# Turning the probabilities of short query blocks in pairs, with zero-padded copies of v, and a new order of all steps

## Time and profile before

| | us |
|---|---|
| median of 3 runs | 584.26 (583.56 to 584.96) |
| the profiled execution | 582.71 |
| its span in the profile | 580.9 |
| PE busy | 528.3 (91%) |
| DVE busy | 448.6 (77%) |
| ACT busy | 413.1 (71%) |
| POOL busy | 349.5 (60%) |

### The profile page before, as it was taken

How to read it: one execution, slowest core, us unless ns; L and a number is a source line. 1 busy time by engine, 2 the same in 40 slices (tenths; PEclk the granted TensorE clock), 3 DMA queues, 4 the chain that set the end, 5 groups by cost and what they waited for, 6 DMA issues and landing times.

```text
span 580.9 us, 22355 instructions
## 1 busy us (share of the span) xinstructions
PE 528.3 (91%) x8180; PEld 451.6 (78%) x8180; DVE 448.6 (77%) x2842; ACT 413.1 (71%) x1004; POOL 349.5 (60%) x358
## 2 busy tenths in 40 slices
PE   4676768999999999999999999999999999989953
PEld 3454647888888888888888888888888888868841
DVE  2799887897897997999998979888989899322114
ACT  3788768867777687867877677778866787566541
POOL 3568456974538565755566645756475648575762
PEclk9678788999999999999999999999999999999995
DMA  7453441000001000110003000200010000000000
GB/s 203 140 173 121 149 143 40 21 2 21 3 3 38 21 3 2 39 39 2 4 2 94 3 3 3 57 21 3 3 39 21 2 21 2 2 19 2 2 18 18
DMA packets 21949, 21.85 MB, mean 38 GB/s; under 512 B 1872, under 2 KB 19792, under 8 KB 21840
## 3 DMA queue, kind: packets, MB, share of 16 engines
q1 hardware_dynamic: 21840, 20.42, 11.5%
HBM read 18.32 MB, written 2.10 MB: 35 GB/s over the span
## 4 chain that ended last, share of the span: by engine, by line
PE 41%; POOL 7%; DVE 5%; issue 4%; ACT 1%; POOLq 0%; DVEq 0%; ACTq 0%
PE ps_o L867 15%; PE ps_z L851 14%; POOL h_lo L522 4%; PE ps_misc L746 3%; PE ps_pt L814 3%; POOL acc L543 2%; PE ps_s L794 2%; PE ps_misc L824 1%; PE ps_misc L754 1%; PE ps_misc L729 1%; DVE taken L959 1%; DVE next L954 1%; ACT h_raw L670 1%; DVE gate_part L998 0%; POOL rstd L561 0%
## 5 line engine op out<-in xcount | busy, mean ns | idle before, releaser
L522 POOL TENSOR_TENSOR h_lo<-h_raw,h_hi 128x512 f16<-128x512 f32 x128 | 148.6, 1161 | 109.1 <-ACT h_raw L670 106.9
L867 PE MATMUL ps_o<-w_hi,h_lo 128*128 128x256 f16 x512 | 139.8, 273 | 5.7 <-POOL h_lo L522 4.9
L851 PE MATMUL ps_z<-x1t_hi,w_lo 128*128 128x256 f16 x512 | 140.5, 274 | 0.1
L851 PE MATMUL ps_z<-x1t_lo,w_hi 128*128 128x256 f16 x512 | 140.1, 274 | 0.0
L851 PE MATMUL ps_z<-x1t_hi,w_hi 128*128 128x256 f16 x512 | 140.0, 273 | 0.0
L867 PE MATMUL ps_o<-w_hi,h_hi 128*128 128x256 f16 x512 | 139.6, 273 | 0.0
L867 PE MATMUL ps_o<-w_lo,h_hi 128*128 128x256 f16 x512 | 139.6, 273 | 0.0
L666 ACT ACTIVATE h_hi<-ps_z 128x512 f16<-128x512 f32 x128 | 75.8, 592 | 69.2 <-PE ps_z L851 69.2
L959 DVE MATCH_REPLACE8 taken<-next,taken 128x64 f32<-128x64 f32 (+4 forms) x480 | 110.6, 243 | 0.2 <-issue 0.2
L543 POOL TENSOR_TENSOR acc<-go_sb,acc 128x512 f32<-128x512 f32 x56 | 71.4, 1275 | 31.1 <-ACT go_sb L680 30.9
L954 DVE MAX8 next<-taken 128x8 f32<-128x64 f32 (+4 forms) x480 | 85.4, 244 | 0.0
(11 more groups left out here) (138 smaller groups left out, 1001.2 us busy)
## 6 DMA issues: line engine op xcount, KB each, us to landing
w_raw<-in_w1t SPq DMA_DIRECT2D x8, 512.0 KB, 4.0
w_raw<-in_w2t SPq DMA_DIRECT2D x8, 512.0 KB, 5.0
xt_sb<-in_xt SPq DMA_DIRECT2D x8, 256.0 KB, 4.2
x_sb<-in_x SPq DMA_DIRECT2D x8, 256.0 KB, 3.4
xa_sb<-in_xt SPq DMA_DIRECT2D x7, 256.0 KB, 3.2
out<-out_sb SPq DMA_DIRECT2D x7, 256.0 KB, 3.5
ctx_sb<-in_ctx_w SPq DMA_DIRECT2D x8, 128.0 KB, 2.2
itok_sb<-in_itok SPq DMA_DIRECT2D x8, 128.0 KB, 2.8
```

The source lines that it names most:

```text
L522: nc.gpsimd.tensor_tensor(h_lo[:, e % 2, 2 * z:2 * z + 2, :], h_raw[:, z, :, :], h_hi[:, e % 2, 2 * z:2 * z + 2, :], ALU.subtract)\
L851: last = pe.matmul(ps_z[z][:, d * UT:(d + 1) * UT], w[:, e, c, at:at + P], x[:, c, :], start=n == 0, stop=n == len(terms) - 1)
L867: last = pe.matmul(ps_o[e % 2][:, b * D:(b + 1) * D], h[:, e % 2, c, b * SEQ:(b + 1) * SEQ], w[:, e, c, :], start=n == 0, stop=n == len(te ...
```

## The change

- `turn_probs`, half 0, makes two transposes where it made four: blocks 0 and 1 lie in columns 0 to 127 of `p_sb` and are turned together, blocks 2 and 3 too. Half 1 makes the same four transposes, in the order of blocks 4, 6, 5, 7 (`TURNED`).
- `copy_probs`, half 0, copies 128 partitions by 256 columns in place of 64 by 512. `pt_sb` has 6 columns of blocks in place of 8.
- After a turn in pairs the keys of block 0 are rows 0 to 63 and those of block 1 rows 64 to 127. `attend` multiplies the same 128 rows once with `v_pad[:, 0]` (v of keys 0 to 63 in rows 0 to 63, zeros below) and once with `v_pad[:, 1]` (the same v in rows 64 to 127, zeros above). The number and shape of its products stay.
- A new step `move_v`, once per unit, on ACT: two DMAs from `v_sb` to the two halves of `v_pad`, 64 partitions by 2176 bytes each (139 KB). `v_pad` has one buffer. The step waits for the unit's v (`v_copied`) and for all `attend` of the unit before (`pv_ready`). Every `attend` waits for both DMAs (`s_pad`).
- The output rows now come in the order of blocks 0, 2, 1, 3, 4, 6, 5, 7. `copy_ot` puts them back and needs four instructions of 128x128 in place of two of 128x256.
- POOL clears `v_pad` (1088 columns) in place of `pt_sb` (2048 columns) at the start.
- All slot numbers are new. No step besides `move_v` is added or taken away.

```diff
-    "shift0": 0.75, "shift1": 0.25, "shift2": 0.5, "shift3": -1.25, "scores": -6.75, "copy_scores": -7, "exp": 4.75,
...
+    "move_v": 8.75, "shift0": 0.75, "shift1": 0, "shift2": 0.5, "shift3": -1.25, "scores": -6.75, "copy_scores": -6.5,
...
 LAST = STEADY | {
+    "shift0": 2.5, "shift1": 2.25, "shift2": 1.25, "shift3": 0.5, "scores": -7.5, "exp": 3, "select": 1,
+    "turn_probs": 7, "copy_probs": 6.5, "turn_probs2": 8.75, "copy_probs2": 8.5, "attend": 11, "gate_sums": 40.75,
...
+    "gate_out": -1, "turn_q4": 88.5, "to_q4": 86.75, "move_v": 12.25, "q": -8.25, "v": 106.75, "spread_q": -8.5,
...
+PT_FROM, PT_COLS = (0, 2), (2, HALF)
+TURNED = (0, 2, 1, 3)
...
+        v_pad = sb("v_pad", [P, 2, UB * HEADS, VW])
...
                 elif name == "copy_probs":
                     k, half = args
-                    rows = P if half else P // 2
+                    at, cols = PT_FROM[half], PT_COLS[half]
...
                     act.activation(
-                        pt_sb[0:rows, k % 2, :, HALF * half:HALF * (half + 1), :].rearrange("p h j q -> p j h q"),
-                        ps_pt[0:rows, :].rearrange("p (j h q) -> p j h q", h=HG, q=QB), ACT.Copy)\
+                        pt_sb[:, k % 2, :, at:at + cols, :].rearrange("p h j q -> p j h q"),
+                        ps_pt[:, 0:cols * P].rearrange("p (j h q) -> p j h q", h=HG, q=QB), ACT.Copy)\
                         .then_inc(pt_copied, 1)
+                elif name == "move_v":
+                    act.wait_ge(v_copied, v + 1)
+                    wait(act, pv_ready, TILES * v)
+                    if v == 0:
+                        act.wait_ge(pool_const, 1)
+                    act.dma_start(v_pad[0:64, 0, :, :], v_sb[0:64, v % RING, :, :]).then_inc(s_pad, 16)
+                    act.dma_start(v_pad[64:P, 1, :, :], v_sb[0:64, v % RING, :, :]).then_inc(s_pad, 16)
...
                     for c in range(CD):
-                        last = act.activation(ot_sb[:, c, :], ps_misc[:, c * UT:(c + 1) * UT], ACT.Identity,
-                                              bias=bv_sb[:, c:c + 1])
+                        for r in range(2):
+                            last = act.activation(
+                                ot_sb[:, c, :].rearrange("p (f i r q) -> p f i r q", r=2, i=2, q=QB)[:, :, :, r, :],
+                                ps_misc[:, c * UT:(c + 1) * UT]
+                                .rearrange("p (f r i q) -> p f r i q", r=2, i=2, q=QB)[:, :, r, :, :],
+                                ACT.Identity, bias=bv_sb[:, c:c + 1])
...
-                    for i in range(HALF):
-                        at = prob_at(HALF * half + i)
+                    for i in range(PT_COLS[half]):
+                        at = i * P if half == 0 else prob_at(HALF + TURNED[i])
                         last = pe.transpose(ps_pt[:, i * P:(i + 1) * P], p_sb[:, k % 2, at:at + P], ident[:, :])
...
+                    pe.wait_ge(s_pad, 32 * (v + 1))
                     for h in range(HG):
-                        for s, rows in enumerate(STRIPS):
+                        of = b * HEADS + g * HG + h
+                        values = v_sb[:, v % RING, of, :]
+                        for rows, head, at, right in ((STRIPS[0], h, 0, v_pad[:, 0, of, :]),
+                                                      (STRIPS[1], h, 0, v_pad[:, 1, of, :]),
+                                                      (STRIPS[2], h ^ SH, 2, values), (STRIPS[3], h ^ SH, 4, values)):
                             last = pe.matmul(ps_misc[rows, h * VW:(h + 1) * VW],
-                                             pt_sb[:, k % 2, h ^ SH * (s // 2), 2 * s:2 * s + 2, :]
-                                             .rearrange("p j q -> p (j q)"),
-                                             v_sb[:, v % RING, b * HEADS + g * HG + h, :], start=True, stop=True)
+                                             pt_sb[:, k % 2, head, at:at + 2, :].rearrange("p j q -> p (j q)"),
+                                             right, start=True, stop=True)
```

## The result

| | before | after |
|---|---|---|
| median us (lowest to highest), 11 runs each | 583.36 (580.81 to 584.96) | 589.02 (584.68 to 592.33) |
| ratio to before, 95% interval | | 1.0096 [1.0069, 1.0124] |
| the profiled execution | 582.71 | 592.33 |
| its span | 580.9 | 590.5 |
| first expert step | 91.4 | 101.1 |

Forecast were 580.0 us and a range of 574.0 to 584.0. The profiled execution of after is the longest of its 11, 3.3 us over the median. So its span is read for where the time lies, and the medians for how much it is.

A forecast was written before the change was run, and what follows sets the result against it. PE was taken as the bound from the first expert step (91.4 us) to 507 us, DVE as setting the start. Terms -5.9 + 0 + 2.0 + 0 - 0.3 = -4.2 took the median 584.26 to 580.1, predicted 580.0, range 574.0 to 584.0.

The forecast's parts named there:

- Transposes, -5.9: PE, first expert step to 507 us: two fewer transposes a tile save 0.22 us in each of 27 tiles, 5.9 us.
- what leaves PE here leaves the span: From 91.4 to 507 us PE is busy 412.5 of 415.6 us, so PE time saved there shortens the span.
- PE time saved turns into other waits: Rival, 91.4 to 507 us: half the PE gain may go to waits for p_sb, pt_sb and x1; 583.3 us, chance 0.11.
- Copies on ACT, 0: copy_probs 0.11 to 0.21 us less a tile, copy_ot 0.45 us more a unit, hidden behind expert steps after the first unit.
- `move_v` on ACT, 0: Two DMA issues a unit, 0.94 us of ACT's queue, just covered before the next unit's L1; upper end 1.5 us.
- Unit 7, +2.0: PE's attend there stands 2.7 us for the copies of v, net +2.2, taken as +2.0; ends +1.3 and +4.6.
- The start, 0: Up to the first expert step, set by DVE: 6.2 us of waits removed, 6.2 us of losses added; ends -4.5 and +4.
- Half the losses and all gains: Low end for the time up to the first expert step: only half the losses come true, all gains do; given as -4.5.
- landing at 5 us, gains halved: High end for the time up to the first expert step: copies of v land after 5 us, half the gains; given as +4.
- The last stretch, -0.3: From 507 us on: PE's 3.3 us of waits for h_low stay, turn_x2 stops waiting its 0.2 us; -0.3 in all.
- The size of a copy: A copy of v taken as 139 KB, landing 2.4 us after issue, 2.2 x 139/128; bounds 1.7 and 5.0.
- the copies of v come too late: Rival, units 0 and 7, attend right behind move_v: landing at 5.0 us in place of 2.4 gives 586.9 us, chance 0.10.

The follow-up runs named there:

- before_short: Kernel before in its own order, half 0 with two transposes and a 256-column copy, blocks 2 and 3 left out: 581.48 us, ratio 0.9977.
- after_early: Kernel after with move_v moved earlier in unit 0 (slot 0.8) and in unit 7 (slot 8.75): 582.24 us, ratio 0.9977.
- u7_early: Kernel after with only unit 7's move_v earlier, slot 12.25 to 8.75: 586.83 us, ratio 1.0063.
- u0_early: Kernel after with only unit 0's move_v earlier, slot 10.75 to 0.8: 583.15 us, ratio 0.9995.
- order_only: Kernel before with all slot numbers of after and no move_v: 586.6 us, ratio 1.0076.
- body_only: Body of after in the order of before, move_v behind copy_v0 in unit 0, slot 8.75 elsewhere: 585.6 us, ratio 1.0047.

## Why the prediction was wrong

The result can be told as three steps, in ratios: the new order +0.0076, the body in the new order with its copies in time 0.9977 - 1.0076 = -0.0099, the late copies +0.0119. In us that is 4.4 - 5.8 + 6.9 = 5.5. The steps add up to +0.0096 by the way they are formed, each from one kernel to the next; what each is worth is the finding. The stretch has the same steps in the profiles: 407.9, then 410.3, 405.0 and 408.0. The forecast had 0 for the order in the start, nothing for it in the stretch, and +2 for the copies.

- *Transposes, -5.9.* The price on PE was right, 0.22 us from start to start for the group of two, and 5.3 us come out of the stretch where DVE is light (406.9 to 401.6), and in the new order (410.3 to 405.0, with the rest of the new body). In the old order 1.4 came out. So "what leaves PE here leaves the span" did not hold for 5.9 us less in the old order. DVE's 359 of 415.6 us looked like 14% of room, but in `before_short` DVE itself waits for PE 12.0 us before `normalise` alone, so part of that room is not free. That an order tuned to one balance has little slack per step is how I read it; no run shows it step by step. This is the mechanism of the rival "PE time saved turns into other waits", seen but given 0.11.
- *Copies on ACT, 0.* Right: 382 and 366 ns, and PE's waits in the stretch of `after_early` name none of them.
- *`move_v` on ACT, 0.* Right, and for another reason: the issues take 0.47 to 1.05 us each, but beside ACT's instructions, as the ACT timeline above shows (issue at 35.12 for 0.56, `copy_scores` at 35.44).
- *Unit 7, +2.0.* Right in the mechanism, and within its ends of +1.3 and +4.6 in size: PE waited 2.2 us. With the copy early the time between the first expert steps of units 6 and 7 fell from 58.0 to 54.8 us in the profiles, 3.2 us, so the wait costs about 1 us more than it lasts; the medians of `u7_early` have 1.9.
- *The start, 0.* This is the step that failed, twice. First the copy: DVE was to wait 3.3 us before the first `normalise`, with a landing from 2.4 us on, and waited 6.5, since one copy landed after 5.1. The term's own ends had slips as well. "Half the losses and all gains" is 3.1 - 6.2 = -3.1 and not -4.5; "landing at 5 us, gains halved" is 6.2 + 2.6 - 3.1 = +5.7 and not +4. With +5.7 here and +4.6 in unit 7 the same sum ends at 588.4 us, not far from what came. Second the gains: 6.2 us of DVE's waits were to go. DVE's waits up to the first expert step, before, and in `u0_early` where the late copy is gone (total, times, longest):
```profile
DVE w_ms L1037 <- PE ps_o L877: 4.2, 3, 3.3
```
```profile
DVE w_ms L1056 <- PE ps_o L896: 4.0, 5, 1.1
DVE rsum L998 <- PE ps_misc L844: 1.8, 4, 0.8
DVE t L1008 <- PE ps_misc L761: 1.7, 1, 1.7
DVE p_sb L987 <- ACT ps_s L629: 1.5, 1, 1.5
```

  The three waits for `w_sum` of 4.2 us, one of them 3.3, are now five that sum to 4.0, those of 2.1 and 1.3 are 1.7 and 1.5, and 1.8 us before `normalise` are new. So the 6.2 us of gains did not come, and without the late copy the start is 91.7 us, before 91.4. Moving one `w_scale` behind two stages moves the wait to the next.

  The late copy is nearly all of the longer start: with it 98.6 us (`u7_early`), without it 91.7 (`u0_early`).
- *The order in the stretch, no term.* The forecast priced the new order in the start alone. `order_only` has 2.4 us more in the stretch than before.
- *The last stretch, -0.3.* Right within what can be read: 3.2 us of waits for 3.3.
- *The size of a copy.* The profile counts 136.0 KB for 64 x 2176 bytes, in the unit in which the loads have 128.0, so the 2.4 us should have been 2.2 x 136/128 = 2.3; this changes nothing.

The rival "the copies of v come too late" named the place, the price in unit 0 and the point from which it decides (3.7 us to landing), and got 0.10. The 0.49 of the DMA engines in the start was counted for it, but that is the mean of 91 us and not the 0.97 of the three that mattered. Against it stood landings of 1.7 and 2.2, medians over a run whose DMA engines are at 0.06 most of the time. Its 586.9 assumed 5.0 us at both places; it was 5.1 in unit 0, and in unit 7 PE's wait of 2.2 us fits the 2.4 of the median. Against the measured 589.0 it lacks the order's 2.4 us in the stretch (407.9 to 410.3 with the old body), and the start cost about 7 us where it had 4.2 (98.6 for 91.4); unit 7 cost less than its 4.6.

Open: why the order costs the old body 2.4 us in the stretch, step by step (it lies in units 1, 3 and 4: 0.8, 0.4 and 1.0 us between their first expert steps and the next unit's); why the start of `body_only` is 97.9; why the last packets of the late copy moved after 39 us, when the DMA engines were mostly idle. The 9.7 us of the profiled start also hold something that is none of the change: the first k projection, 8 products, takes 3.78 us there and 1.99 before, with the same granted clock in both rows, and the first scores are 1.9 us later for it. `u7_early` has the steps of after in its start, but the short form, and its start is 98.6 for 101.1; `after_early` with the long form and `u0_early` with the short one have 94.5 and 91.7. How much of these 2.5 and 2.8 us is due to the form is not shown: `before_short` has the long form too, and its start is 91.4 as before. PE timelines, after and before, then their windows:
```profile
9.88 3.78 PE L744 MATMUL ps_misc<-xt_sb,wk_sb 128*128 128x256 f32 x8 [0.93 <-ACT qt_sb L593]
```
```profile
9.79 1.99 PE L729 MATMUL ps_misc<-xt_sb,wk_sb 128*128 128x256 f32 x8 [0.93 <-ACT qt_sb L589]
```
```profile
9.90:13.60 3.70, 3.70 (x8) 2.51 (x8) 0.00 (x0) 0.00 (x0) 2.33 (x4) 1.00 0.97 207
```
```profile
9.80:11.70 1.90, 1.90 (x8) 1.43 (x8) 0.00 (x0) 0.00 (x0) 1.81 (x4) 1.00 0.75 108
```
Six of the 17 profiles have the long form, of old bodies and new. No run here tells what sets it.

## What to carry to other kernels

When an added transfer becomes the last thing that a full engine waits for, read the DMA share and the issues in the very microseconds where it will run, not the mean of the stage, and issue it as soon as its source is there: here one slot number was worth 5.9 us. When work is taken off the bound engine, look at how much of the next engine's time is free between its own waits, and test it by leaving some of its work out, with the change and without it: 31 us off DVE were worth 1.0 us of the stretch before, and 4.9 us with two transposes fewer. And price a new order as a change of its own, run with the old body.

## What was not expected of the hardware

- A DMA issued from ACT occupies ACT's queue for 0.47 to 1.05 us (in after) but did not keep ACT from computing: a `copy_scores` starts 0.32 us after an issue of 0.56 us began.
- The same copy of 136 KB from SBUF to SBUF took 2.4 us as the median of 8, but 5.1 us where two loads of 256 KB were issued beside it and the next weights before it landed, and 3.3 us with one such load and the weights behind it. The tail of the weights before was in flight in both.
- The same 8 fp32 products took 1.99 or 3.78 us at a granted clock that the rows give as 1.00 in both.
